# Half-size expert tiles, a start that loads one layer first, and a new order of ScalarE's copies in a two-layer decoder kernel

## What is computed

```
layer 0:  x += window_attention(ln(x))        # 16 heads of 16, |i-j| <= 32
          x += cross_attention(ln(x), ctx)    # 77 context rows an item, padded keys masked
          x += experts(ln(x))                 # 8 experts, top 2 a token: 256 -> 512 -> 512 -> 256, gelu
layer 1:  x += causal_attention(ln(x))
          x += cross_attention(ln(x), ctx)    # one mask for all items
          x += quantised_ffn(ln(x))           # gate/up/down, weights rounded to 4 bits in blocks of 32
```

## Time and profile before

| what | value |
|---|---|
| median of 3 runs | 2432.71 us (2432.21 to 2432.74) |
| the profiled execution | 2430.9 us, of which the span from first to last instruction is 2428.9 us |
| mean granted TensorE clock | 0.952 |
| busy share of the span | PE 89%, PEld 66%, DVE 52%, ACT 36%, POOL 28% |
| first attention, up to item 0's first instruction on TensorE | 0 to 48.71 us |
| experts, first tile | 778.77 to 816.73 us |
| experts, the 38 other tiles | 816.73 to 1356.27 us |
| second attention, up to item 0's first instruction on TensorE | 1364.59 to 1391.69 us |
| the second attention's steps, then the quantised ffn | 1391.69 to 2428.9 us |

### The profile page before, as it was taken

The page is one execution under the profiler, slowest core; times in us unless marked ns, Lnnn a source line. Parts: engine busy times, 40 slices in busy tenths (PEclk is TensorE's granted clock), DMA queues, the critical chain, the costliest instruction groups (busy, mean ns, idle before and its releaser), DMA issues. The chain is left out here.

```text
span 2428.9 us, 46335 instructions
## 1 busy us (share of the span) xinstructions
PE 2154.3 (89%) x15496; PEld 1607.6 (66%) x15496; DVE 1260.6 (52%) x5376; ACT 885.9 (36%) x1511; POOL 670.3 (28%) x1192
## 2 busy tenths in 40 slices
PE   3799999999993999999999679999999999799869
PEld 2577777666662788888888456767766666344348
DVE  3677776555542210000011367788766766439974
ACT  0344444444441122222222124444544444237510
POOL 2355555134444000000000234444322211003410
PEclk9899999998985999999999779999999999899989
DMA  4332233222223555455544343333222222000013
GB/s 132 116 104 99 99 108 99 92 85 77 95 70 136 203 204 199 182 193 205 192 182 186 91 133 106 119 123 111 94 80 86 80 90 76 9 0 1 0 44 96
DMA packets 206739, 266.86 MB, mean 110 GB/s; under 512 B 57893, under 2 KB 194762, under 8 KB 201610
## 3 DMA queue, kind: packets, MB, share of 16 engines
q1 hardware_dynamic: 192986, 233.91, 27.7%
q0 software_dynamic: 9264, 27.01, 3.6%
q10 hardware_dynamic: 4352, 4.20, 0.5%
HBM read 123.21 MB, written 30.93 MB: 63 GB/s over the span
## 5 line engine op out<-in xcount | busy, mean ns | idle before, releaser
L1629 ACT ACTIVATE moe_h<-moe_h_ps,moe_weights 128x256 f32<-128x256 f32 x312 | 131.0, 471 | 442.9 <-PE moe_h_ps L1600 358.5
L1600 PE MATMUL moe_h_ps<-moe_h,moe_weights 128*128 128x256 f32 x1248 | 277.7, 381 | 0.0
L1659 DVE TENSOR_TENSOR moe_y<-moe_y_ps,moe_weights 128x512 f32<-128x512 f32 x39 | 27.0, 692 | 482.4 <-PE moe_y_ps L1611 482.4
L1081 ACT ACTIVATE causal_prob<-causal_ps 128x768 f32<-128x768 f32 (+1 forms) x192 | 169.1, 881 | 248.5 <-PE causal_ps L1264 247.5
L1600 PEld LDWEIGHTS moe_h_ps<-moe_h,moe_weights 128*128 128x128 f32 x1248 | 235.6, 191 | 30.8
L2031 PE MATMUL ffn_prod_ps<-x_sb,ffn_weights 128*128 128x512 f32 x480 | 210.6, 598 | 9.7 <-ACT ffn_sig_q L2017 7.0
L832 DVE CUSTOM_DVE_ANT_0 causal_masked<-causal_ps,causal_causal_mask 128x256 bf16<-128x256 f32 (+1 forms) x512 | 152.1, 353 | 67.6 <-PE causal_ps L1228 67.2
L1561 POOL DMA_DIRECT2D moe_y_dram<-moe_y x39 | 29.6, 760 | 560.1 <-DVE moe_y L1659 560.1
L2031 PEld LDWEIGHTS ffn_prod_ps<-x_sb,ffn_weights 128*128 128x128 f32 x480 | 90.9, 191 | 127.1 <-issue 110.0
L832 DVE CUSTOM_DVE_ANT_0 window_masked<-window_ps,window_window_mask 128x160 bf16<-128x160 f32 x512 | 135.3, 320 | 63.1 <-PE window_ps L1228 61.3
L1584 PE MATMUL moe_h_ps<-moe_rowsT,moe_weights 128*128 128x256 f32 x624 | 143.6, 384 | 1.2 <-DVE moe_rowsT L1648 1.2
(11 more groups left out here) (347 smaller groups left out, 4504.9 us busy)
## 6 DMA issues: line engine op xcount, KB each, us to landing
moe_weights<-moe_w_in SPq DMA_DIRECT2D x39, 2180.0 KB, 8.5
q_pair<-window_q_parts SPq DMA_DIRECT2D x256, 128.0 KB
q_pair<-causal_q_parts SPq DMA_DIRECT2D x256, 128.0 KB
k_pair<-window_k_parts SPq DMA_DIRECT2D x128, 128.0 KB
k_pair<-causal_k_parts SPq DMA_DIRECT2D x128, 128.0 KB
moe_rows<-moe_slots_dram SPq DMA_DIRECT2D x39, 256.0 KB, 2.8
moe_y_dram<-moe_y POOLq DMA_DIRECT2D x39, 256.0 KB, 2.5
k_pair<-window_k_parts SPq DMA_DIRECT2D x128, 38.5 KB
```

The costliest lines, as they stand in the source:

```text
L1081: nc.scalar.activation(out, src, ACT.Exp).then_inc(expd, 1)
L1600: op = nc.tensor.matmul(h2_ps[:, f // 2, (f % 2) * TM:(f % 2) * TM + TM], w2[:, k, f * P:f * P + P], h1[:, k, :], start=(k == 0), stop=(k ...
L1629: nc.scalar.activation(out[:, f, :], psum[:, f // 2, (f % 2) * TM:(f % 2) * TM + TM], ACT.Gelu, bias=bias[:, f:f + 1]).then_inc(done, 1)
L1659: nc.vector.tensor_tensor(y[r][:], y_ps[:, r, :].rearrange("p (s d) -> p s d", s=TS), b3.unsqueeze(1).to_broadcast([P, TS, D]), ALU.add).t ...
```

## The change

TM becomes 128, so MT becomes 71; the ring of tile buffers has 4 places and the ring of output banks 2 (`YR`). VectorE's work on raw weights is cut in three and spread over tiles 2, 3 and MT-7 to MT-2. In `attention` the loads are put in order of need (layer 0's weights, then x or the gathered rows' wait, the context, layer 1), item 0's statistics are ahead of the constants and of the rest, the context is turned after step 0 with ScalarE copying two tiles at a time, the bias products are in slot 5 of steps 0 and 1, masks of layer 1 are prepared after step 0. x is loaded in five parts, and only items 0 and 1 are waited for at first. Memsets of `q_pair` and `k_pair` are gone. Normalisation of the next item goes from slot 6 to slot 7. ScalarE's exponentials 0 and 6 of cross layers go behind the copies `xT` and `oT`. Outputs are turned bank 1 first, and the waits for bank 0 stand between the two.

```diff
-TM = 256
+TM = 128
...
+                load_layer(0)
+                if load:
+                    x_view, _, x_second, x_loaded = load
+                    sp.dma_start(x_sb[:, ST:TILES // 4, :], x_view[:, ST:TILES // 4, :]).then_inc(x_second, 16)
+                if merge:
+                    sp.wait_ge(got_in[0], 64)
                 for L in crosses:
...
+                for r in range(1, NL):
+                    load_layer(r)
+                if load:
+                    for n in range(1, 4):
+                        quarter = slice(n * TILES // 4, (n + 1) * TILES // 4)
+                        sp.dma_start(x_sb[:, quarter, :], x_view[:, quarter, :]).then_inc(x_loaded, 16)
...
                 if merge:
                     gather(0, 0)
+                else:
+                    layernorm(0, 0)
+                constants()
+                if route:
+                    route_constants()
+                if merge:
+                    layernorm(0, 0)
                     gather(1, 1)
-                layernorm(0, 0)
-                if merge:
                     gather(2, 2)
-                if crosses:
-                    pool.wait_ge(ctx_copied, CTX_TILES * len(crosses))
...
-                        if i == 1 and active(ref, -1):
+                        late = bool(merge) and ref == 0
+                        if i == 4 and late:
+                            for n in range(4):
+                                merge_rows(1, 1, n)
+                        if i == (4 if late else 1) and active(ref, -1):
                             stats(t + 1, ref + 1)
...
-                        if i == 6 and active(ref, -1):
+                        if i == 7 and active(ref, -1):
...
+                        if i == 5 and ref < NL:
+                            widen(ref)
+                    if ref == 0:
+                        dve.wait_ge(consts, 1)
+                        for r in range(1, NL):
+                            scale_layer(r)
+
+                nc.vector.memset(recip[:], 0.0)
                 if merge:
+                    scale_layer(0)
...
                 stats(0, 0)
...
+                if not merge:
+                    scale_layer(0)
...
-                        if i == 7 and active(ref, 3):
-                            act.wait_ge(oT_mm, t - 2)
-                            nc.scalar.activation(oT[:], xT_ps, ACT.Copy).then_inc(oT_ev, 1)
-                        if active(ref, 2):
+                        if i == 7 and active(ref, 3) and not (active(ref, 2) and layer_at(ref, 2).pairs == 2):
+                            keep_oT(t)
+                        wide = active(ref, 2) and layer_at(ref, 2).pairs == 2
+                        turned_first = wide and (i == 0 and active(ref, 0) or i == 6 and active(ref, 3))
+                        if active(ref, 2) and not turned_first:
                             exponentials(t, ref, i)
                         if i == 0 and active(ref, 0):
                             act.wait_ge(xT_mm, t + 1)
                             nc.scalar.activation(xT[:], xT_ps, ACT.Copy).then_inc(xT_ev, 1)
+                        if i == 6 and turned_first:
+                            keep_oT(t)
+                        if turned_first:
+                            exponentials(t, ref, i)
...
+                    if ref == 0:
+                        copy_context()
+
+                act.wait_ge(begun, 1)
+                nc.scalar.activation(warm[:], ln["eps"][:, 0:1], ACT.Exp)
...
-                            wait(pe, m_ev, upto(t, ref, 1, 2) - (1 if active(ref, 1) else 0))
                             wait(pe, v_ev, upto(t, ref, 0))
                             wait(pe, added, upto(t, ref, 4))
-                            wait(pe, oT_ev, upto(t, ref, 4))
-                            for s in range(ST):
+                            for s in reversed(range(ST)):
+                                if s == 0:
+                                    wait(pe, m_ev, upto(t, ref, 1, 2) - (1 if active(ref, 1) else 0))
+                                    wait(pe, oT_ev, upto(t, ref, 4))
...
+                        if i == 5 and ref < NL:
+                            bias_product(ref)
+                    if ref == 0:
+                        turn_context()
...
-RING = 3
+RING = 4
+YR = 2
...
-                        if not first_turn(j):
-                            pe.wait_ge(y_done, j - (RING - 1))
+                        wait(pe, y_done, j - (YR - 1))
...
+                    def beside(j):
+                        if j == 0:
+                            compact()
+                        for m in range(3):
+                            if j == (2, 2, 3)[m]:
+                                find_scales(m)
+                            if j == (3, MT - 7, MT - 7)[m]:
+                                divide(m)
+                            if j == (MT - 6, MT - 6, MT - 5)[m]:
+                                round_off(m)
+                            if j == (MT - 5, MT - 4, MT - 4)[m]:
+                                clip(m)
+                            if j == (MT - 3, MT - 3, MT - 2)[m]:
+                                rescale(m)
...
-                for n in range(4):
-                    tiles = slice(n * TILES // 4, (n + 1) * TILES // 4)
-                    sp.dma_start(x_sb[:, tiles, :], x_view[:, tiles, :]).then_inc(x_loaded, 16)
-                sp.wait_ge(x_loaded, 64)
...
+                sp.dma_start(x_sb[:, 0:ST, :], x_view[:, 0:ST, :]).then_inc(x_first, 16)
```

More of the change, by code:

```diff
@@ new lines, in _ @@
+                if load:
[3 more added lines that the diff above has]
+                if route:
+                    with nc.allow_non_contiguous_dma(reason="eight columns"):
+                        sp.dma_start(gate_w[:], route.weight.rearrange("(k p) e -> p k e", p=P)).then_inc(route_loaded, 16)
+                        sp.dma_start(gate_b[:], route.bias.rearrange("(o e) -> o e", o=1).to_broadcast([P, NE]))\
+                          .then_inc(route_loaded, 16)
@@ L495, in store, with halve_masks @@
+                def halve_masks():
+                    for r, L in enumerate(layers_in):
+                        if L.mask_key is None:
+                            continue
+                        sp.wait_ge(scaled[r], 1)
+                        nat = L.mask_nat[-1][:]
+                        for part in rows_of:
+                            for half in range(2):
+                                sp.dma_start(L.mask_key[part, half, :], nat[rows_of[half], :]).then_inc(halved, 16)
                 def store(t, ref):
@@ L1518, in views, with tiles @@
                         w[:, B1_AT:B2_AT], w[:, B2_AT:B3_AT], w[:, B3_AT:WPACK])
[L1520 to L1527 removed]
+            def tiles(engine, tile, beside=lambda j: None):
+                turns = MT // RING - 2
+                for j in range(RING):
+                    tile(j, j, 0)
+                    beside(j)
+                with engine.Fori(0, turns) as turn:
                     for k in range(RING):
                         tile(turn * RING + (RING + k), k, turn + 1)
[L1530 to L1533 removed]
+                for j in range(RING * (turns + 1), MT):
+                    tile(j, j % RING, j // RING)
+                    beside(j)
             first_turn = lambda j: isinstance(j, int) and j < RING
@@ L1698, in _, with divide @@
-                    tiles(dve, tile, {0: compact, 1: find_scales, 2: divide, MT - 3: round_off, MT - 2: rescale})
+                        link(nc.vector.tensor_reduce(wmax[:, part], blocks(m), AX.X, ALU.max, apply_absolute_value=True))
+                        link(nc.vector.tensor_scalar(wscale[:, part], wmax[:, part], 1.0 / 7.0, LEAST, ALU.mult, ALU.max))
+                        link(nc.vector.reciprocal(winv[:, part], wscale[:, part]))
+                    def divide(m):
+                        link(nc.vector.tensor_tensor(blocks(m), blocks(m), each(winv, m), ALU.mult))
@@ L1703 @@
+                    tiles(dve, tile, beside)
 FI = 768
@@ L2144, in _ @@
             def _(dve):
-                for i in range(2):
-                    nc.vector.memset(k_pair[i][:].bitcast(F32), 0.0)
                 dve.wait_ge(filled, 1)
```

334 lines of the change are left out of this document (186 added, 148 removed).

## The result

The changed kernel takes 2330.26 us (median of four runs, 2326.99 to 2332.67) where the kernel before, measured beside it, takes 2432.72: ratio 0.9576, 95% interval 0.956 to 0.9593. The forecast was 2341, with 2316 to 2400 as its range. The profiled execution has 2332.67 us and a span of 2331.1, against 2428.9 before: 97.8 less.

The account below looks back on a forecast made before the run. TensorE's own stream was taken to bound the experts and nearly the attention steps, with other idle time in starts. From 2430.9 us, terms of -27.5 - 27 - 9 - 28 = -91.5, plus 1.8, gave 2341.2 us; range 2316 to 2400.

Parts of the forecast that it names:

- Experts, -27.5: Expert stage: 128-row tiles take 7.35 us at 0.1125 us a record; -20.4 after the first tile, -7 in it.
- The transfers hidden: Expert loop: each tile's 2436 KB takes 6.3 us, under 7.35; issue and landing are hidden with 3.1 us to spare.
- rival B: Expert loop: transfers set the tile as flow falls below 388 KB/us or landing grows; 2422 us, half as bad 2381; chance 0.13.
- Rival D: Expert loop: a 0.190 us weight load sets the record, 11.07 us a tile; +260, 2602 us; chance 0.05.
- First start, -27: First attention: item 0 reaches TensorE at about 15.5 instead of 48.71 us; displaced context and bias work leaves net -27.
- rival C: Starts and cross layers give half of their 64 us as displaced work blocks something; 2373 us; chance 0.12.
- Second start, -9: Second attention: item 0 waits for gathering alone, 14.7 us instead of 27.10, -12.4; net -9 after later costs.
- Normalisation in slot 7, 0: Attention steps: normalisation some 0.7 us later costs 0; bounds -3 to 0.73 us in each of 62 steps.
- Cross layers, -28: Cross-layer steps: waits for xT -11.5, for oT -11.6, for maxima -5.7; later exponentials free; together -28 after 0.8 for takeovers.
- Sum: Whole kernel: experts -27.5, first start -27, second start -9, cross layers -28; total -91.5, giving 2341.2 us.

Follow-up runs that it names:

- ring3: Changed kernel with three weight buffers instead of four, and VectorE's raw-weight work moved by a tile or two to fit; 2500.43 us in its one run.
- sp_late: Changed kernel with SP issuing the second layer's loads behind item 0's rearranging DMAs, rest of x and gate weights behind item 1's; ratio 0.9609 to the kernel before.
- after_again: The changed kernel itself, unaltered, measured again in the third session; 2351.23 us, ratio 0.9632 to the kernel before.
- bias_late: Changed kernel with the small bias product's widening copy in slot 3 instead of 5 and its result's copy behind slot 7; ratio 0.9606 to the kernel before.
- x_starts: Kernel before with only both attentions' new starts and normalisation in slot 7 (TM = 256, RING = 3, old ScalarE order); ratio 0.9876, -31.9 us.
- slot6: Changed kernel with the normalisation back in slot 6 instead of slot 7; ratio 0.9642 to the kernel before.
- best: Changed kernel with SP's loads later, bias product's copies apart, raw-weight work spread evenly and normalisation in slot 6; 2334.05 us, ratio 0.9573 to the kernel before.

## Why the prediction came out right, step by step

- **Experts, -27.5.** Right. Record 0.1116 us (0.1125), tile 7.31 (7.35), first tile -7.1 (-7). VectorE's stalls in the loop are 4.6 us, 2.05, 1.54, 0.64 and 0.39, at the places named (forecast 4.6; its parts, 2, 1.3 and twice 0.7, add up to 4.7). Alone the experts' part gives -30.3, and 2.4 are given back in turning the raw weights behind the last tile, which the forecast didn't have: -27.9.
- **The transfers hidden.** Right in kind, and ring3 shows what carries it: without the lead of the fourth buffer the kernel is 170 us slower, slower than before the change. Two of its parts were mis-sized against each other: from the end of the products to the issue of weights 2.6 us (906.63 to 909.22), not 3.1, and landing 9.5 (the median in the changed kernel), not 8.5. Issue to turning is 12.0 us (909.22 to 921.25), so 2.5 us were to spare where I had 3.1. The flow of 325 GB/s lies under the burst's 388, as rival B had it, but cost nothing.
- **Rival D, the weight load sets the record.** Fell. Loads still stand at 190 ns and 492 of 516 us busy, beside records every 112 ns. The Trainium skill, "TensorE: Matmul & The Clock Gate", section "The mechanism", lists overlap with loads to other row groups only; the trace disagrees with this for these full-height float32 products, as it did before. The same section also says that a load to the background weight buffer is pulled ahead of running matmuls. The prediction left that out; it leaves room for what the trace has, but no run here shows that buffer.
- **First start, -27.** The sum is right (-26.8 alone at item 16), but two of its reasons are not, so that is partly luck. "At worst 2 us of delay" by SP's queue was worked out from bytes at 388 KB/us. What counted was the time that issues take: 13.4 us of them lay between the context's last load and q's rearrangement, and sp_late took 5.3 us out by order alone. And the low clock was in no term. Steps 1 and 2 had it before as well, 0.76 and 0.83, now 0.74 and 0.84. In step 0 it is now 0.88, and was 0.98. Step 3 has 0.84 and takes 24.29 us in the changed kernel's first trace, where item 16 is 24.4 us earlier than before; in after_again it has 1.00 and takes 21.32, much as in the kernel before (21.69). Item 0 was earlier than forecast, 14.88 for 15.5. Steps 0 to 2 took 63.3 us, over the mark of 60 set for rival C, whose price wasn't paid.
- **Second start, -9.** Item 0 -12 to -13.5 (-12.4 forecast). Items 32 to 36 cost 4.8 where 3.4 was left for them (-12.4 to -9), since the bias product's waits fall beside VectorE's gathered sums; bias_late gets back 2.7. With some 2 us for the longer causal steps of x_starts that makes -6.6.
- **Normalisation in slot 7, 0.** Near enough in size. A cost that I hadn't thought of, the gathers' issues beside it, 0.03 to 0.05 us longer each, would make some 2 us in the causal layer; slot6 and best gave nothing back in the step, so that the kernel's time follows is not shown.
- **Cross layers, -28.** Measured -30.5 alone. The split was off: the copies of the outputs and rows in front are worth 1.0 us a padded step where I had 0.77 (23.1 us over 30 steps), bank 1 first nothing there. I priced three waits as if independent; the wait for the maxima was one that the next wait took over. The exponentials' lateness is free, as forecast.
- **Sum.** -91.5 forecast, -93.5 as the parts alone, -88 to -102 as a whole. The misses in the terms (2.5 us too little for the cross layers, 2.4 too much for the second start) cancel, which is luck. That the first measurement lay 11 us below the forecast goes with items 20 to 31: they took 207.9 us in its trace, and 215.4 to 223.9 in the six later traces of the changed kernel and its variants.

Not settled: why causal steps with gathers took 0.6 to 0.8 us more in the later sessions in every kernel, and what decides in items 20 to 31 which clock is granted and whether TensorE waits for `xT`. In the causal steps TensorE's, VectorE's, ScalarE's and POOL's instructions are as long in after_again as in the first trace; the difference is idle time.

## What to carry to other kernels

When tiles shrink and their weights don't, count the lead of an issue over its use in tiles and close the loop around it before looking at the rate: one more buffer was worth 170 us here. At a start, count what stands in the issuing queue in the time that its issues take, which grows behind large loads, and not in bytes alone; put behind the first item's own transfers all that it doesn't need. Of several waits in one step only the chain counts: removing one is worth what the next doesn't take over, and an edit in the order of one engine shows in a step's length before it shows in a run's time.

## What was unexpected in the hardware

- TensorE's granted clock was 0.74 to 0.88 in steps 0 to 2, where it is busy 13 to 18 of 20 to 22 us (0.64 between 36 and 58 us in sp_late), and so partly at its lower level of 1.2 GHz. In the padded steps with routing it moves from run to run, and I found no cause: the same eleven steps took 207.9 or 223.9 us, and a step with TensorE busy 20.96 of 21.23 us had 0.84.
- A float32 record of 128 columns against changing 128x128 weights passes every 0.1116 us although each load's record is 190 ns long, nearly the pace of a transpose (0.108).
- SP takes 0.4 to 0.5 us for the issue of most loads. The eight-column gate weights took 2.9 us behind three 1 MB loads and 0.38 with nothing in front; those three took 3.5 together.
- POOL's issue of an indirect gather takes 0.97 us in steady causal steps, and 1.02 with VectorE's normalisation in slot 7.
